# Joining and transposing attention's maxima some tiles later, and splitting x1 from PSUM, in an attention and FFN layer

## Time and profile before

| | |
|---|---|
| median of 3 runs | 2956.26 us (2952.41 to 2957.12) |
| the profiled execution | 2954.24 us |
| its span in the trace | 2952.1 us |
| mean granted PE clock | 0.986 of full |
| busy: PE, DVE, ACT, POOL | 97%, 95%, 87%, 13% |

### The profile page before, as it was taken

The page is one execution under the profiler, slowest core; times in us unless marked ns, Lnnn a source line. Parts: engine busy times, 40 slices in busy tenths (PEclk is TensorE's granted clock), DMA queues, the critical chain, the costliest instruction groups (busy, mean ns, idle before and its releaser), DMA issues. The chain is left out here.

```text
span 2952.1 us, 66175 instructions
## 1 busy us (share of the span) xinstructions
PE 2870.8 (97%) x27022; PEld 891.0 (30%) x27022; DVE 2792.1 (95%) x3142; ACT 2578.5 (87%) x4656; POOL 396.4 (13%) x426
## 2 busy tenths in 40 slices
PE   8989999999999999999999999999999999989998
PEld 5522222222222222222222222222222222246665
DVE  8989999999999999999999999999999999658787
ACT  5747999999999999999999999999999999945555
POOL 7830000000000000000000000000000000136553
PEclk9978999999999999999999999999999999989999
DMA  5421111111111111111111111111111111133431
GB/s 195 149 96 32 34 34 34 34 35 34 34 34 34 34 34 34 34 34 34 34 34 34 34 34 34 34 34 34 34 34 34 34 34 34 56 88 86 115 93 37
DMA packets 120850, 145.77 MB, mean 49 GB/s; under 512 B 52576, under 2 KB 86752, under 8 KB 120544
## 3 DMA queue, kind: packets, MB, share of 16 engines
q1 hardware_dynamic: 120256, 141.51, 16.3%
q10 hardware_dynamic: 288, 0.01, 0.0%
HBM read 105.78 MB, written 35.13 MB: 48 GB/s over the span
## 5 line engine op out<-in xcount | busy, mean ns | idle before, releaser
L884 ACT ACTIVATE probs<-st_ps 128x512 f32<-128x512 f32 x4096 | 2228.4, 596 | 147.7 <-PE st_ps L799 78.6
L908 DVE TENSOR_REDUCE tile_max<-s_ps 128x1 f32<-128x1024 f32 x2048 | 2327.8, 1209 | 2.6 <-PE s_ps L785 2.4
L810 PE MATMUL o_ps<-probs,kept_v 128*17 128x256 f32 x16384 | 1283.4, 385 | 22.6 <-ACT sums L871 22.6
L785 PE MATMUL s_ps<-k,q 64*128 64x512 f16 x4096 | 1251.9, 386 | 17.5 <-PEq L88 7.4
L799 PE MATMUL st_ps<-q,k 64*128 64x512 f16 x4096 | 1247.4, 382 | 0.0
L810 PEld LDWEIGHTS o_ps<-probs,kept_v 128*17 128x17 f32 x16384 | 273.7, 95 | 887.3 <-issue 455.5
L799 PEld LDWEIGHTS st_ps<-q,k 64*128 64x128 f16 x4096 | 272.7, 93 | 870.4 <-ACT probs L884 867.0
L987 POOL TENSOR_SCALAR max_scaled<-neg_max_t 128x32 f32<-128x32 f32 x64 | 18.5, 290 | 2304.6 <-DVE neg_max_t L919 2304.6
L785 PEld LDWEIGHTS s_ps<-k,q 64*128 64x128 f16 x4096 | 233.2, 94 | 77.2 <-DVE tile_max L908 62.9
L1183 ACT ACTIVATE silu<-g_ps 128x512 f32<-128x512 f32 x96 | 57.3, 597 | 121.6 <-PE g_ps L1103 121.6
L1278 POOL TENSOR_TENSOR h_low<-hidden,h_high 128x512 f16<-128x512 f32 x96 | 113.2, 1189 | 130.5 <-ACT h_high L1167 130.5
(11 more groups left out here) (100 smaller groups left out, 1283.1 us busy)
## 6 DMA issues: line engine op xcount, KB each, us to landing
q<-q_parts SPq DMA_DIRECT2D x192, 128.0 KB
k<-k_parts SPq DMA_DIRECT2D x192, 128.0 KB
x_t<-in_x_t SPq DMA_DIRECT2D x16, 512.0 KB, 7.2
q_parts<-parts SPq DMA_DIRECT2D x32, 256.0 KB, 2.6
k_parts<-parts SPq DMA_DIRECT2D x32, 256.0 KB, 2.6
heads_out<-sums SPq DMA_DIRECT2D x256, 32.0 KB, 2.0
kept_v<-heads_out SPq DMA_DIRECT2D x16, 512.0 KB, 5.6
kept_v<-inverses_out SPq DMA_DIRECT2D x32, 256.0 KB
```

The source lines that it names most:

```text
L785: mm = pe.matmul(s_ps[g % 2][:, j * BANK:(j + 1) * BANK], q[h % 2][FIRST, r // KW * P:(r // KW + 1) * P], k[h % 2][FIRST, at:at + BANK], s ...
L810: mm = pe.matmul(o_ps[c * 32:c * 32 + VM, at:at + HALF], t["kept"][:, h, kt, :], probs[(h * KT + kt) % RING][:, c * BANK + at:c * BANK + a ...
L884: act.activation(probs[(h * KT + kt) % RING][:, c * BANK:(c + 1) * BANK], st_ps[n % ST][:, :], ACT.Exp, scale=scale).then_inc(exp_done, 1)
L908: dve.tensor_reduce(tile_max[h % 2][:, r // KW, r % KW:r % KW + 1], s_ps[g % 2][:, :], AX.X, ALU.max).then_inc(s_read, 1)
```

## The change

Two independent parts.

In attention `head_maxima` is split. For head h the join now follows the maximum of the next head's first tile, and the transposition the maximum of its second. `LEAD` goes from 8 to 10. The join thus stands behind n = 22 of the loop, the transposition behind n = 23, where both stood before.

In `finish` ACT makes both `x1_high` straight from `t_ps`, and only then, each behind the corresponding `x1_low`, both `x1_t`. DVE's `low` reads `t_ps` in PSUM, scales it and subtracts `x1_high` in one scalar_tensor_tensor, in place of a tensor_tensor on two tiles in SBUF. PE's wait in front of the gate stays on `x1_low_done` in the branch taken.

```diff
-    LEAD = 8
+    LEAD = 10
...
-            def head_maxima(h):
+            def join_maxima(h):
                 i = h % 2
                 dve.wait_ge(s_read, (h + 1) * MAXES)
                 wait(dve, max_turned, h - 1)
                 dve.tensor_reduce(neg_max[i][:, 0:QT], tile_max[i][:, :, :], AX.X, ALU.max,
                                   negate=True).then_inc(head_max, 1)
+
+            def turn_maxima(h):
+                i = h % 2
                 dve.wait_ge(head_max, h + 1)
                 wait(dve, max_cut, CUTS * (h - 1))
                 dve.transpose(neg_max_t[i][:, :], neg_max[i][:, :]).then_inc(max_turned, 1)
...
-            head_maxima(0)
+            join_maxima(0)
+            turn_maxima(0)
...
                     if g < TILES:
                         maximum(g)
-                        if g % MAXES == MAXES - 1:
-                            head_maxima(g // MAXES)
+                    if g % MAXES == 0 and g <= TILES:
+                        join_maxima(g // MAXES - 1)
+                    if g % MAXES == 1 and g <= TILES + 1:
+                        turn_maxima(g // MAXES - 1)
...
-                    pe.wait_ge(x1_low_done, KD * (c + 1))
+                    pe.wait_ge(x1_t_done if wide else x1_low_done, KD * (c + 1))
...
             def take_transposed(c):
                 for kd in range(KD):
                     act.wait_ge(turned, KD * c + kd + 1)
+                    act.activation(x1_high[:, kd, :], t_ps[:, kd, :], ACT.Copy, scale=X1_SCALE
+                                   ).then_inc(x1_high_done, 1)
+                for kd in range(KD):
+                    act.wait_ge(x1_low_done, KD * c + kd + 1)
                     act.activation(x1_t[:, kd, :], t_ps[:, kd, :], ACT.Copy, scale=X1_SCALE
                                    ).then_inc(x1_t_done, 1)
-                    act.wait_ge(x1_t_done, KD * c + kd + 1)
-                    act.copy(x1_high[:, kd, :], x1_t[:, kd, :]).then_inc(x1_high_done, 1)
...
                     dve.wait_ge(x1_high_done, KD * c + kd + 1)
-                    dve.tensor_tensor(x1_low[:, kd, :], x1_t[:, kd, :], x1_high[:, kd, :],
-                                      ALU.subtract).then_inc(x1_low_done, 1)
+                    dve.scalar_tensor_tensor(x1_low[:, kd, :], t_ps[:, kd, :], X1_SCALE, x1_high[:, kd, :],
+                                             ALU.mult, ALU.subtract).then_inc(x1_low_done, 1)
```

## The result

The changed kernel takes 2931.75 us, the median of four runs (2930.65 to 2934.98), where the kernel before took 2955.0 beside it (2952.41 to 2957.12): a ratio of 0.9924, 95% interval 0.9906 to 0.9941. On another chip it took 2930.54 (five runs, 2929.24 to 2931.21), a ratio of 0.9913 (0.99 to 0.9927). The forecast was 2930. The profiled execution is one of 2930.65, its span 2928.5, which is 23.6 less than before.

The account below looks back on a forecast made before the run. DVE was taken to pace attention, and PE's wait for the second `x1_low` to cost 0.92 us at 11 chunk boundaries. 2954.24 - 17.0 + 2.3 - 10.3 = 2929.2, given as 2930 us; range 2922 to 2940, chance 0.80.

Parts of the forecast that it names:

- What sets the pace: DVE paces attention, 1.13 us a loop step against 1.09 for PE and ACT; 0.92 us lost at each of 11 boundaries.
- Join and transposition: In attention, moving the two DVE instructions apart saves 0.27 us a head, 63 times: 17.0 us, bounds 13.9 and 20.2.
- The two waits: In attention, DVE's waits on its own results before the join and before the transposition: 0.11 us each, 0.22 a head.
- each like the reciprocal: In attention, if join and transposition each cost the reciprocal's 0.10 us, 0.20 stays and 0.24 goes a head.
- The 0.08 us that I put down to the drain: In attention, the rest of a head's 0.62 us between maxima, ascribed to the drain of the sums, for which PE's `times_v` waits.
- Two tiles in front: Before attention's first exponential, two more tiles cost 2.35 us; two later loop steps give back 0.08: together +2.3 us.
- The slack of the maxima: In attention, read-back maxima land at 1373.7, SP's next stack is at 1376.33: some 2.6 us of slack, left by the change.
- The slower rival: In attention, maxima come back too late and every head begins with a wait; a 4 us longer path gives 3017; chance 0.03.
- The low part: At 11 chunk boundaries, each new low takes 0.75 us and the gate follows at once: gain 10.3 us, bounds 0 and 10.3.
- ACT's delay: At chunk boundaries, x1_t behind the lows makes the first silu 0.4 us late; counted 0, uncovered 4.4 us.
- my upper bound of 10.3: At the chunk boundaries, the most that the new low could gain, in us; the lower bound was 0, if the gate still waits.
- The three terms: Over the whole kernel: -17.0 us for join and transposition, +2.3 for two tiles in front, -10.3 for the low part.

## Why the prediction was right

**What sets the pace.** DVE in attention, one wait of PE at eleven chunk boundaries: both confirmed, the first also by taking 0.10 us away from DVE and getting 0.10 us a head.

**Join and transposition.** Forecast 0.27 us a head, 17.0 in all. Measured 0.25: 15.5 over heads 1 to 61 and, if it gains as much, 0.25 more in head 0; head 62 gains nothing by it (36.07 us in the split with eight tiles too). 15.8 in all. The two waits I had put at 0.22 together, and one of them measured alone gives 0.125. What stays is 1.22 - 1.13 = 0.09 us for the join and 1.26 - 1.13 = 0.13 for the transposition, of which the next start wins back 0.03: 0.19 of the 0.44. I had said 0.17. The bound "each like the reciprocal", 0.20 staying and 0.24 going, was the better one. The 0.08 us that I put down to the drain are there in both kernels: of the steps from maximum to maximum, the one behind n = 3 is 1.20 us and the next 1.14, right behind PE's wait of 0.36 us for ACT's `drain`.

**Two tiles in front.** Forecast +2.3, measured +2.4 in front, -0.2 in head 62 and about -1.0 in head 0: some +1.2. What is mis-sized here is the 2.35 us for the two tiles: I took their price from tiles at half the clock (1.174 us each) and did not ask what head 0, which begins at that clock too, would gain by starting later.

**The slack of the maxima.** Right for the change, which leaves it as it was, and misread in size. The 2.0 us to landing count from an issue's start, and I added them to its end: in the head that I read the maxima landed at 1373.14 and not at 1373.7. And one head is not all: the way from transposition to landing is 5.4 us in the median head of the kernel before and 7.5 in the longest, where the first exponential comes only 1.5 us behind the landing. Since a waiting head needs 0.57 of these, the smallest slack there is 0.9 us, where I had 2.6; with 2.26 us less a third of the heads waited. A slack behind a DMA has to be read as the smallest over many heads. The slower rival is thus nearer than I put it, though no head of the changed kernel is late.

**The low part.** Forecast -10.3, measured -10.4 in chunks 1 to 11. Each low takes 0.69 us, not 0.75. ACT's delay: I expected the first silu 0.4 us late and no cost. It starts 2727.73 - 2726.47 = 1.26 us behind the gate, where it was 1.07, so 0.2 us late, and a chunk's length, 19.93 us, is that of the chunks which never had the wait. The first chunk is where the account fell short. Its first gate gained nothing, as forecast, since PE is at its branch; but its lows held up POOL's `h_low`, for which PE waited at two products of `down`, 0.5 us each, and that went. I had counted the low only where the gate waits for it, and so the gain of this part is about 1 us above my upper bound of 10.3.

**What the sum did not have.** +2.4 us in front of attention's first maximum, -0.5 to the first gate (16.9 to 18.3 us over the traces) and some -0.2 in head 0 are scatter. The three terms came to about -15.8 + 1.2 - 11.4 = -26.0 us where I had -25.0. The rest of the 23.6, +2.4, is this scatter and chunk 0, which shows 0.6 us less than the 1.0 I give it (about the scatter of its length in one kind of kernel), and could have been 3 us either way. So the two pacemakers and the large terms are right by their mechanism, while the agreement of 2930 with 2931.75 and 2930.54 to within 2 us is partly luck: the split gave 1.2 us less than forecast, the lead cost 1.1 less, the low gave 1.1 more, and these and the scatter offset one another.

## What to carry to other kernels

On an engine that sets the pace, look for an instruction that waits for its own engine's result right in front of it, and put other work between; here that was worth 0.12 us each time, twice a head. An elementwise step of DVE that falls under GpSimd work was better fed from PSUM, where the data already was, than from a second SBUF tile, and the gain lay on both sides: look also for what waits for GpSimd. And when work is moved nearer to the consumer behind a DMA, test one step at a time: eight tiles of lead were too few, nine just enough, and with ten no head was late in any trace, while the median alone could hardly tell nine from ten.

## What the hardware showed that I had not expected

PE runs at half its clock through the tiles in front, and the clock rises only some microseconds into the loop, at a moment that differs from run to run. By stretches (start and length; PE, PEld, DVE, ACT, POOL; granted clock), the kernel before, whose first exponential is at 233.71:

```profile
236.00:240.00 4.00, 3.90 (x25) 0.56 (x23) 3.25 (x4) 2.62 (x5) 0.00 (x0) 0.50 0.13 52
240.00:244.00 4.00, 4.00 (x40) 0.78 (x36) 3.21 (x4) 2.71 (x6) 0.00 (x0) 0.78 0.12 51
```

and the changed one, whose first exponential is at 238.50:

```profile
238.00:242.00 4.00, 3.65 (x15) 0.51 (x11) 3.94 (x4) 3.29 (x7) 0.00 (x0) 0.50 0.13 53
242.00:246.00 4.00, 4.00 (x37) 0.78 (x36) 3.43 (x4) 2.63 (x5) 0.00 (x0) 0.79 0.13 52
```

0.50 is 1.2 GHz, 1.00 is 2.4; the clock is at 0.50 in both from before the first maximum. A mean of 0.78 over 4 us means a rise about 2.3 us before the stretch's end, at 241.7 in the one and 243.7 in the other: 8.0 and 5.2 us behind the first exponential, but 56.5 and 56.1 behind attention's first maximum. The two more tiles in front, 2.4 us, thus did not move the rise, and head 0 runs that much less at half its clock.

What this is worth is read from kernels of one kind whose rise came at different moments. The changed kernel's head 0 is 37.33 us long with the rise 5.2 us behind the first exponential and 37.46 with 5.5; with nine tiles it is 37.71 with 6.1 and 38.37 with 7.6; unsplit, 38.18 with 6.7 (ten tiles) and 38.74 with 8.0 (eight). Each microsecond by which the rise comes sooner is 0.4 to 0.5 us of head 0, so of the 2.4 us of the two tiles about 1.0 comes back.

The rise also scatters by itself, between 55.8 and 57.8 us behind the first maximum in twelve of the thirteen traces and 53.9 in the split with eight tiles. Another source of scatter is the stage in front: attention's first maximum came between 185.0 and 191.0 us, at 187.6 and at 185.0 for the very same program. These are of the size of the spread of 3 to 8 us between runs, and more than what the lead costs; that they make up all of it is not shown.
